# S4D convolution, the head of the prologue: powers of the exponential, angles, cosine and the placing of D

## The reference, cut to what matters

```python
dt = jnp.exp(log_dt)                                   # (128,)
A = -jnp.exp(log_A_real) + 1j * A_imag                 # (128, 64)
dtA = A * dt[:, None]
Cs = Cc * (jnp.exp(dtA) - 1.0) / A
K = 2.0 * jnp.einsum('hn,hnl->hl', Cs, jnp.exp(dtA[:, :, None] * jnp.arange(2048))).real
y = irfft(rfft(u * mask, 4096) * rfft(K, 4096))[..., :2048] + u * mask * D[:, None]
out = x + y * mask                                     # x (64, 128, 2048), float32
```

## Time and profile before

| what | us |
|---|---|
| median of three runs | 859.32 |
| lowest and highest run | 857.62, 860.59 |
| the profiled execution | 858.43 |
| its span, first to last instruction | 856.6 |
| TensorE matmuls busy | 819.1 (96%) |
| VectorE busy | 733.3 (86%) |
| GpSimd busy | 648.2 (76%) |
| ScalarE busy | 618.4 (72%) |

### The profile page before, as it was taken

How to read it: one execution, slowest core, us unless ns; L and a number is a source line. 1 busy time by engine, 2 the same in 40 slices (tenths; PEclk the granted TensorE clock), 3 DMA queues, 4 the chain that set the end, 5 groups by cost and what they waited for, 6 DMA issues and landing times.

```text
span 856.6 us, 22236 instructions
## 1 busy us (share of the span) xinstructions
PE 819.1 (96%) x6174; PEld 754.2 (88%) x6174; DVE 733.3 (86%) x2016; ACT 618.4 (72%) x1716; POOL 648.2 (76%) x720
## 2 busy tenths in 40 slices
PE   0689999999999999999999999999999999999997
PEld 0579989888999999999999999999999999999996
DVE  8978988888888888888888888888888888888886
ACT  3667777777777777777777777777777777777774
POOL 7897777777777777877787777778787877777761
PEclk9999999999999999999999999999999999999999
DMA  5055787777777777777877777787777777777775
GB/s 110 5 115 135 183 200 180 190 186 181 189 193 183 193 186 196 186 195 189 192 189 184 194 183 196 187 195 189 192 192 186 198 184 195 184 195 186 198 186 135
DMA packets 161367, 152.76 MB, mean 178 GB/s; under 512 B 13504, under 2 KB 161216, under 8 KB 161216
## 3 DMA queue, kind: packets, MB, share of 16 engines
q1 hardware_dynamic: 161344, 152.48, 72.2%
HBM read 84.08 MB, written 67.30 MB: 177 GB/s over the span
## 4 chain that ended last, share of the span: by engine, by line
PE 87%; DMA 4%; DVE 3%; POOL 2%; SPq 2%; issue 1%; ACT 1%; DVEq 0%; POOLq 0%; ACTq 0%
PE y L1006 13%; PE y L1008 13%; PE y L1007 13%; PE y L1043 12%; PE v L1023 10%; PE xt_even L991 6%; PE xt_odd L991 6%; DMA xall<-in_x_dram 4%; PE v L1006 3%; PE v L1007 3%; PE v L1008 3%; PE y L1001 2%; PE y L1002 2%; SPq L345 1%; DVE q L748 1%
## 5 line engine op out<-in xcount | busy, mean ns | idle before, releaser
L545 ACT ACTIVATE room<-v 64x192 f32<-64x192 f32 (+1 forms) x768 | 235.8, 307 | 170.2 <-DVE v L899 153.3
L899 DVE SCALAR_TENSOR_TENSOR v<-v,RV,mid 128x192 f32<-128x192 f32 (+2 forms) x512 | 192.4, 376 | 55.0
L899 DVE SCALAR_TENSOR_TENSOR mid<-room,RV,v 128x192 f32<-128x192 f32 (+2 forms) x512 | 184.4, 360 | 41.2 <-ACT room L545 21.9
L1006 PE MATMUL y<-thi,uhi 128*128 128x256 f32 x512 | 186.4, 364 | 0.0
L895 DVE COPY_PREDICATED xall<-mask,y 128x512 f32<-128x512 int32 x256 | 176.0, 736 | 1.4 <-issue 1.4
L1006 PE MATMUL y<-fhi,zhi 128*128 128x256 f32 x512 | 154.6, 302 | 1.8 <-DVE zlo L722 1.6
L1008 PE MATMUL y<-thi,ulo 128*128 128x256 f32 x512 | 144.5, 282 | 0.0
L1008 PE MATMUL y<-fhi,zlo 128*128 128x256 f32 x512 | 144.0, 281 | 0.0
L1007 PE MATMUL y<-tlo,uhi 128*128 128x256 f32 x512 | 144.0, 281 | 0.0
L1007 PE MATMUL y<-flo,zhi 128*128 128x256 f32 x512 | 144.0, 281 | 0.0
L524 POOL TENSOR_TENSOR room<-W,B 128x512 f32 (+1 forms) x127 | 141.9, 1117 | 0.0
(11 more groups left out here) (179 smaller groups left out, 1945.4 us busy)
## 6 DMA issues: line engine op xcount, KB each, us to landing
xall<-in_x_dram SPq DMA_DIRECT2D x256, 256.0 KB, 4.7
out_dram<-xall SPq DMA_DIRECT2D x254, 256.0 KB, 3.4
traw<-krows SPq DMA_DIRECT2D x128, 128.0 KB, 2.9
NXY<-B SPq DMA_DIRECT2D x2, 512.0 KB, 6.3
out_dram<-xall SPq DMA_DIRECT2D x4, 128.0 KB, 2.4
krows<-ksb SPq DMA_DIRECT2D x8, 1.0 KB, 2.0
krows<-ksb SPq DMA_DIRECT2D x8, 4.0 KB, 4.0
krows<-ksb SPq DMA_DIRECT2D x8, 11.0 KB, 3.8
```

What stands on the lines that cost most here:

```text
L545: return act.activation(dst, src, ACT.Copy)
L899: return dve.scalar_tensor_tensor(out=out, in0=src, scalar=RV[:, k:k + 1, h], in1=other, op0=ALU.mult, op1=ALU.add)
L1006: pe.matmul(o, a_hi, b_hi, start=start, stop=False, skip_group_check=True)
```

## The change

Magnitudes are computed by the series for three powers (k = 0, 4, 8) and the others by three squarings. ScalarE rounds the exponents too. Angles take two steps instead of three. ScalarE makes the cosine itself: 1 - 2 sin^2 of the half angle by a Square and an Identity, into `cs`. `lim` gets a buffer of its own. `combine` goes; `lim` and `lre` are one product each. `x_low(0, 0)` is moved ahead of the products. D is placed straight into `dvec` (now 128 x 16) by one strided DMA of 128 single elements behind the x loads; GpSimd sets `dvec` to -1 before and adds 1 after, and `add_d` reads `dvec`. The broadcast load of D and the tiles `dall`, `dsel`, `own` go.

```diff
+STRIDE = 4
+NEXP = len(POWERS[::STRIDE])
...
-        dall = sb("dall", [P, H])
-        dsel = sb("dsel", [P, 8])
-        own = sb("own", [P, 8, SQ])
-        dvec = sb("dvec", [P, 8])
+        dvec = sb("dvec", [P, SQ])
+        lim_flat = sb("lim", [P, NPOW * N])
+        cs = view(wide, npn)
-        ang, lim = view(wide), view(wide, npn)
+        ang, lim = view(wide), view(lim_flat[:])
...
@@ SP @@
-            sp.dma_start(dall[:], D.rearrange("(a h) -> a h", a=1).broadcast_to([P, H])).then_inc(s_len, 16)
...
             sp.wait_ge(s_pool0, 1)
+            sp.dma_start(dvec[SQ - 1:P:SQ, :], D.rearrange("(g c) -> c g", c=8),
+                         allow_slow_non_contiguous=True).then_inc(s_d, 16)
             sp.dma_start(krows.ap()[:, CHUNK:CHUNK + PAD], zpad[:]).then_inc(s_kz, 16)
...
@@ GpSimd @@
+            link(pool.memset(dvec[:], -1.0))
...
-            pool.wait_ge(s_len, 48)
+            pool.wait_ge(s_len, 32)
             pool.tensor_copy(flen[:], ilen[:])
-            link(pool.tensor_copy(dsel[:], ident[:, SQ - 1:P:SQ]))
...
-            for n in (4, 2, 1):
-                halved(dvec, n)
-            pool.engine_nop().then_inc(s_d, 1)
+            pool.wait_ge(s_d, 16)
+            pool.tensor_scalar(dvec[:], dvec[:], 1.0, None, ALU.add).then_inc(s_d, 1)
             pool.wait_ge(s_norm, 2)
...
@@ ScalarE @@
-            for k in range(1, len(POWERS[::2])):
+            for k in range(1, NEXP):
...
+            act.wait_ge(s_round, 1)
+            act.activation(whole[:, 0:NEXP * N], q2[:, 0:NEXP * N], ACT.Identity, bias=rnd[:, 0:1],
+                           scale=1.0 / math.log(2.0)).then_inc(s_rounded, 1)
+            act.wait_ge(s_rounded, 1)
+            act.activation(whole[:, 0:NEXP * N], whole[:, 0:NEXP * N], ACT.Identity,
+                           bias=rnd[:, 1:2]).then_inc(s_rounded, 1)
             act.wait_ge(s_angles, 1)
...
-            act.activation(sn.rearrange("p k n -> p (k n)"), flat, ACT.Sin)
-            act.activation(sh.rearrange("p k n -> p (k n)"), flat, ACT.Sin, scale=0.5).then_inc(s_sin, 1)
+            act.activation(sh_flat, flat, ACT.Sin, scale=0.5).then_inc(s_sin, 1)
+            act.activation(sn_flat, flat, ACT.Sin).then_inc(s_sin, 1)
+            act.wait_ge(s_sin, 1)
+            act.activation(sh_flat, sh_flat, ACT.Square, scale=math.sqrt(2.0)).then_inc(s_sin, 1)
+            act.wait_ge(s_sin, 3)
+            act.activation(cs.rearrange("p k n -> p (k n)"), sh_flat, ACT.Identity, bias=pw[:, 0:1],
+                           scale=-1.0).then_inc(s_sin, 1)
...
-            act.wait_ge(s_d, 1)
+            act.wait_ge(s_d, 17)
...
@@ VectorE, behind L775 @@
+            n = NEXP * N
+            dve.wait_ge(s_arg, NEXP)
+            reduced(0, k, r, src).then_inc(s_round, 1)
             dve.wait_ge(s_pool0, 1)
             dve.tensor_tensor(ang[:, 1:, :], ang[:, 0, :].unsqueeze(1).broadcast_to([P, NPOW - 1, N]),
                               pw[:, 1:].unsqueeze(2).broadcast_to([P, NPOW - 1, N]), ALU.mult).then_inc(s_angles, 1)
+            dve.wait_ge(s_rounded, 2)
+            dve.wait_ge(s_round, 1)
+            link(reduced(3, k, r, src))
+            link(reduced(4, k, r, src))
+            dve.tensor_scalar(k.bitcast(I32), k, 127.0, float(2 ** 23), ALU.add, ALU.mult)
+            link(dve.tensor_scalar(q, r, 1.0 / math.factorial(7), None, ALU.mult))
+            for d in (6, 5):
+                link(dve.scalar_tensor_tensor(out=q, in0=q, scalar=1.0 / math.factorial(d), in1=r,
+                                              op0=ALU.add, op1=ALU.mult))
+            dve.wait_ge(s_whole, 2)
+            dve.wait_ge(s_angles, 1)
+            for part in (c1, 2 * math.pi - c1):
+                link(dve.scalar_tensor_tensor(out=flat, in0=q1[:], scalar=-part, in1=flat, op0=ALU.mult, op1=ALU.add))
+            dve.tensor_scalar(flat, flat, 3.1415925, -3.1415925, ALU.min, ALU.max).then_inc(s_ang, 1)
+            for d in range(4, 0, -1):
+                link(dve.scalar_tensor_tensor(out=q, in0=q, scalar=1.0 / math.factorial(d), in1=r,
+                                              op0=ALU.add, op1=ALU.mult))
+            link(times_two_k(mag[:, 0:NPOW:STRIDE, :], q.rearrange("p (k n) -> p k n", n=N),
+                             k.rearrange("p (k n) -> p k n", n=N)))
+            dve.tensor_tensor(em1[:], q[:, 0:N], k[:, 0:N], ALU.mult)
+            for d in range(1, STRIDE):
+                new = mag[:, d:NPOW:STRIDE, :]
+                old = mag[:, d - 1:NPOW - 1:STRIDE, :]
+                link(dve.tensor_tensor(new, old, old, ALU.mult))
+            dve.scalar_tensor_tensor(out=em1[:], in0=k[:, 0:N], scalar=-1.0, in1=em1[:], op0=ALU.add, op1=ALU.add)
             dve.wait_ge(s_norm, 1)
             dve.reciprocal(norm, norm).then_inc(s_norm, 1)
-            dve.wait_ge(s_sin, 1)
-            combine(0, NPOW)
+            x_low(0, 0)
+            dve.wait_ge(s_sin, 3)
+            link(dve.scalar_tensor_tensor(out=t1, in0=sh[:, 0, :], scalar=-1.0, in1=mag[:, 0, :], op0=ALU.mult, op1=ALU.mult))
+            dve.tensor_tensor(lim, mag, sn, ALU.mult)
+            dve.tensor_tensor(l1r, em1[:], t1, ALU.add)
+            dve.wait_ge(s_sin, 4)
+            dve.tensor_tensor(lre, mag, cs, ALU.mult).then_inc(s_lam, 1)
...
-            link(dve.tensor_tensor(l1r, em1[:], q1[:, 0:N], ALU.add))
-            x_low(0, 0)
...
@@ add_d @@
-                dve.tensor_tensor(k0, k0, dall[:].rearrange("p (g c) -> p g c", c=8)[:, g, :], ALU.add).then_inc(s_kfin, 1)
+                d0 = dvec[:, g].unsqueeze(2).broadcast_to([P, g.stop - g.start, 8])
+                dve.wait_ge(s_d, 17)
+                dve.tensor_tensor(k0, k0, d0, ALU.add).then_inc(s_kfin, 1)
```

More of the change, by code:

```diff
@@ L162, in s4d_kernel @@
         s_len = sem("s_len")
+        s_round = sem("s_round")
+        s_rounded = sem("s_rounded")
         s_pool0 = sem("s_pool0")
@@ L555, in _ @@
             act.wait_ge(s_arg, 1)
-            for k in range(1, len(POWERS[::2])):
-                act.activation(arg[:, k, :], arg[:, 0, :], ACT.Copy, scale=float(POWERS[2 * k])).then_inc(s_arg, 1)
+            for k in range(1, NEXP):
+                act.activation(arg[:, k, :], arg[:, 0, :], ACT.Copy, scale=float(POWERS[STRIDE * k])).then_inc(s_arg, 1)
             act.wait_ge(s_pool0, 1)
+            act.wait_ge(s_round, 1)
[4 more added lines that the diff above has]
+                           bias=rnd[:, 1:2]).then_inc(s_rounded, 1)
             act.wait_ge(s_angles, 1)
-            act.activation(q1[:], ang.rearrange("p k n -> p (k n)"), ACT.Identity, bias=rnd[:, 0:1],
+            flat = ang.rearrange("p k n -> p (k n)")
+            act.activation(q1[:], flat, ACT.Identity, bias=rnd[:, 0:1],
                            scale=1.0 / (2 * math.pi)).then_inc(s_whole, 1)
@@ L752, in times_two_k @@
                 return dve.scalar_tensor_tensor(out=dst, in0=q, scalar=1.0, in1=two_k, op0=ALU.add, op1=ALU.mult)
[L754 to L761, removed]
             dve.wait_ge(s_prm, 16 * 2)
@@ L778, in _ @@
                               pw[:, 1:].unsqueeze(2).broadcast_to([P, NPOW - 1, N]), ALU.mult).then_inc(s_angles, 1)
-            c1 = 6.28125
[L781 to L802, removed]
@@ L803, in _ @@
-            dve.wait_ge(s_angles, 1)
-            dve.wait_ge(s_whole, 2)
-            take_turns(reduced_angle(0))
-            take_turns(reduced(4, k, r, src))
-            link(reduced_angle(1))
-            link(reduced_angle(2))
-            link(dve.tensor_scalar(flat, flat, 3.1415925, -3.1415925, ALU.min, ALU.max))
-            dve.engine_nop().then_inc(s_ang, 1)
-            series(q, k, r, k)
+            flat = ang.rearrange("p k n -> p (k n)")
+            dve.wait_ge(s_rounded, 2)
@@ L812, in _ @@
             dve.wait_ge(s_norm, 1)
             dve.reciprocal(norm, norm).then_inc(s_norm, 1)
-            link(times_two_k(mag[:, 0:NPOW:2, :], q.rearrange("p (k n) -> p k n", n=N),
-                             k.rearrange("p (k n) -> p k n", n=N)))
-            dve.tensor_tensor(em1[:], q[:, 0:N], k[:, 0:N], ALU.mult)
-            link(dve.tensor_tensor(mag[:, 1:NPOW:2, :], mag[:, 0:NPOW - 1:2, :], mag[:, 0:NPOW - 1:2, :], ALU.mult))
-            link(dve.scalar_tensor_tensor(out=em1[:], in0=k[:, 0:N], scalar=-1.0, in1=em1[:], op0=ALU.add, op1=ALU.add))
@@ L827, in _ @@
             dve.tensor_tensor(t3, l1i, g_re, ALU.mult)
-            link(dve.tensor_tensor(l1r, em1[:], q1[:, 0:N], ALU.add))
             dve.tensor_tensor(t2, l1r, g_re, ALU.mult)
-            dve.tensor_tensor(em1[:], l1r, g_im, ALU.mult).then_inc(s_dve, 1)
-            done[0] += 1
-            x_low(0, 0)
-            dve.wait_ge(s_dve, done[0])
+            link(dve.tensor_tensor(em1[:], l1r, g_im, ALU.mult))
             dve.tensor_tensor(NXY[:, SQ - 1, 1, 0, :], t2, t1, ALU.add)
```

13 lines of the change are left out of this document (2 added, 11 removed).

## The result

| | before | after |
|---|---|---|
| median of six runs | 858.3 | 853.72 |
| lowest and highest | 857.0, 860.59 | 851.0, 854.5 |
| the profiled execution | 858.43 | 853.59 |
| its span | 856.6 | 851.8 |

The ratio is 0.9942, 95% interval 0.9926 to 0.9958: 3.6 to 6.4 us faster. The forecast was faster, 855.3 us, with a range from 853.8. By ratio the forecast (855.3 over 859.32, 0.9953) lies inside the interval; three more runs of the kernel before brought its own median down by 1.0.

The account below looks back on a forecast made before the run. The prediction took the prologue's VectorE chain up to s_lam, then GpSimd's tables, as the bound. Its steps brought s_lam from 24.15 to 20.1, so 859.32 - 4.05 = 855.3 us, range 853.8 to 858.0.

Parts of the forecast that it names:

- The bound: Start of the kernel: VectorE's chain up to s_lam sets the time, each us there a us of the whole.
- Step 1: Up to the reduction: ScalarE's copies, VectorE's clamp and ScalarE's roundings, with VectorE going on at 9.27.
- Step 2: VectorE from 9.27: two reductions, power of two, first term and two terms of the series, until 11.28.
- Steps 3 and 4: Two angle steps and a clamp, s_ang at 13.71; then four series terms, three squarings and the reciprocal, at 17.40.
- Step 5: x_low(0, 0) moved ahead (0.61), then t1, lim, l1r and lre: s_lam at 20.1, 4.05 us earlier.
- What was costed at nothing in the head: ScalarE's sines, Square and cosine, covered by 2.1 and 1.8 us, and D's transfer, hidden with 1.7 us.
- the row that I took: Landing time assumed for D's transfer: 17.1 us, as the zero padding had, from bounds of 11.5 and 17.1.
- (a): ScalarE's Square needs its own table load: still 855.3 at 1.28 us, 856.2 at 2.56 us; chance 0.12.
- (b): D lands late and delays GpSimd's tables, one for one after 19.0; chance 0.03 past 25.7, 0.05 for partial loss.
- (c): Between s_lam and the loop the gain is given back: 857.5 with half lost; chance 0.10.
- the cost of the loop: Loop over the 128 channels, untouched apart from two adds of D: costed at nothing.
- the base: Starting time for the sum: median of three runs, 859.32, 0.9 above the profiled execution's 858.43.

Follow-up runs that it names:

- Experiments 8 and 9: Two variants of the changed kernel: cosine combined by VectorE without Square and Identity, ratio 0.9951; series for six powers with one squaring, ratio 0.9969.
- experiment 10: Changed kernel with a one-column Exp on ScalarE between the sine and Square, forcing a table switch: ratio 0.9931.
- experiment 2: Changed kernel with 4.0 us of idle VectorE products added behind the reciprocal, making the head as long as before: ratio 0.999 to the kernel before.
- experiments 2 and 3: experiment 2, and the changed kernel with x_low(0, 0) moved back behind s_lam: ratio 0.9919, median 852.0.
- experiment 4: Changed kernel with x_low(0, 0) behind s_lam and lim and lre split, the four fine powers first with their own semaphore: ratio 0.9942.
- experiment 7: Changed kernel with D's transfer held back until VectorE's reciprocal is done: ratio 0.9954.

## Why the prediction was right and where it was wrong

**The bound** was read rightly: all that counts is when `s_lam` comes, and the lead is 3.88 there and 3.94 at channel 0.

**Step 1** had VectorE go on at 9.27; it was 9.36: the clamp took 0.37, not 0.27, and the roundings 0.45 each, not 0.43. **Step 2** ended at 11.46 instead of 11.28: half of that lateness is step 1's, half its own. **Steps 3 and 4**: the two angle steps 1.82, the clamp 0.53, four terms 1.53, three squarings 1.07, each within 0.1 of the sum. The end of the reciprocal is where `x_low` starts, 17.57 against 17.40. **Step 5**: `t1` at 18.11 (18.0), `lre` ending at 20.27 (20.1). Experiments 8 and 9 put its two main terms to the test on their own: 1.46 for cosine, 2.23 for the powers. The steps missed by 0.2 us in all, in one direction.

**What was costed at nothing in the head** was nothing: Square and Identity (2.1 us of cover at `t1`, 2.4 at `lre`) and D. D came at about 16.2, a us before the row that I took; it lies between the two bounds, 11.5 and 17.1.

**The rivals.** (a) has no ground: no load came, and a forced one stayed hidden. The Trainium skill, "ScalarE: Activation LUTs", section "What ACT_TABLE_LOAD costs", puts a switch at 2.66 us with a drain; this trace has 1.28 and no drain beside it. With 2.66 in experiment 10, as an estimate, Square would have ended at 18.95 and `t1` would have waited; it didn't, and the measurement decides. (b)'s mechanism is real, and one point fits the price I gave it, but its condition was far off. (c) was posed the wrong way round: I looked only for ways in which the loop could take some of the gain. It also names 10 to 20 us as the stretch in which TensorE idles longest; TensorE does no matmul at all in the first 10 us, where the granted clock is 1.00 as well.

**The step that failed** is the cost of the loop, which I put at nothing, and with it the lower end of the range. In the first pair of profiles the loop added 0.91 us to the head's 3.94, and in the other two profiles of the changed kernel 0.54 and 2.59. Over all seventeen profiles the loop share runs from -1.8 to +3.3 us, which is more than any single term of the sum. I allowed 1.5 us downwards, and even that doesn't come out of my own terms: 0.3 and 1 give 854.0, not 853.8. That the loop's text is unchanged was a reason for a mean of nothing, not for a scatter of nothing, and by the runs above even the mean is doubtful. What makes the scatter is known in the main, TensorE's waits for x; what makes a mean that isn't zero stays open.

The second part is the base. The sum against the profiled execution gave 854.4, 0.8 above what that execution came to. Then I added 0.9 to reach a median of three runs, and three more runs took 1.0 off again. Of runs that scatter by 3.5 us, three don't fix a median to better than about 1 us. This is luck rather than a wrong step: in the four later sets the median of the kernel before is 858.7 to 859.3, close to the 859.32 that I used, and the 858.3 of six runs was low.

In numbers, the forecast was 1.6 us too high (855.3 against 853.72): 1.0 from the base, and just over 0.5 because the medians are 4.6 apart and not 4.05. In that 0.5 the head is 0.1 to 0.2 short and the loop gives 0.6 to 0.7 more than nothing.

## What to carry to other kernels

A chain of dependent VectorE instructions can be summed from the sizes shown within 0.2 us in 13, and a stretch at the start that hands over by one semaphore carries its gain to the loop one for one, within about 0.3 us. When the gain is half a per cent, the range must come from the scatter of the stretch that isn't touched, read from its waits for DMAs in two or more profiles of the same kernel, and not from the chain; and a median of three runs is a base no better than the profiled execution. Before two engines are made to run side by side, look at which inputs lie in SBUF: here the instruction that reads PSUM was the one to put beside GpSimd's products.

## What the runs showed of the hardware

- GpSimd's small products are slowed when VectorE runs a product with two inputs from SBUF beside them: 0.32 us alone or beside `x_low` (one input from PSUM), 0.70 beside products of 448 columns, 0.83 (experiment 2) and 0.97 (experiments 2 and 3) beside products of 704; VectorE's 704 columns went from 0.89 to 1.04. This took half of the gain of experiment 4. The Trainium skill, "SBUF — State Buffer", section "SBUF: two separate sides", describes one pair of ports that either engine locks for a whole instruction, when VectorE has two SBUF inputs and GpSimd reads SBUF. The rows agree that it takes two SBUF inputs and that one instruction holds up the other; that the lock lasts for the whole instruction they don't show (`lim` began 0.29 us before GpSimd's first product ended and lost only 0.15).
- A transfer of 128 pieces of 4 bytes with a stride took 2.5 us to land with no load of x under way (experiment 7), against 1.9 for the same number in a row.
- In an unchanged loop, TensorE's waits for loads differed from execution to execution by up to 1.4 us with the very same kernel (2.0 and 0.6), and the total with them (853.59 and 851.94).
